# Newton's step on GpSimd, the values evicted by ScalarE, the input split one slot later, and new orders in a local-attention transformer on one core

## The chip, the cores and the metric

One NeuronCore of a Trainium2 chip runs the whole program in one launch. The metric is device time in microseconds (us): the median of three runs, and beside it one profiled execution. Engines are named as in the profile: PE (TensorE matmul), PEld (its weight loads), DVE (VectorE), ACT (ScalarE), POOL (GpSimd), SP (SyncE, which issues the DMAs).

## What is computed

The program runs two MoE phases, a recurrence, one attention with a position bias, and twice the same six-layer local transformer. The change lies in that transformer alone. Cut to what matters:

```python
def attn_layer(x, Wqkv, qs, ksc, Wo):               # x: 8 batches of 256 tokens, 128 wide
    q, k, v = split(x @ Wqkv)                       # 16 heads of 64
    q = l2norm(q) * qs;  k = l2norm(k) * ksc        # l2norm: t / max(norm(t), 1e-12)
    q = q*cos*scale + rotate_half(q)*sin*scale      # k with 1/scale
    out = local_attention(q, k, v)                  # windows of 32 tokens, looking one window back
    return out @ Wo
def ffn_layer(x, ...):                              # layer norm, 128 -> 2*341, a*gelu(gate), -> 128
for i in range(6):
    x = attn_layer(shift_tokens(x), ...) + x
    x = ffn_layer(shift_tokens(x), ...) + x
```

## The kernel before: units, slots and written-out orders

A *unit* is one batch with four of the sixteen heads; a layer has 32 units (8 batches by 4 head groups), a phase 192, the two phases 384. Every engine runs the same endless list of *slots*, one new unit per slot; in slot s it works on unit s (u0 in the code), s-1 (u1) and so on down to s-5 (u5). What an engine does inside a slot is a list written by hand (`slot(L, s)`, one per engine), and engines meet only at semaphores (`upto(engine, semaphore, unit)` waits until that unit's step is done). Buffers are mostly double, so that an engine can run ahead of another by a fraction of a slot.

The steps of a unit, with their lines: `project` (PE, L785) multiplies each of the two 128-token tiles t by the q and k weights into PSUM banks A[0], A[1], in three fp32r products each (L49 to L51); `square_of` (ACT, L979) squares a bank; `lengths` (DVE, L1111) sums squares per head; `cosine` and `sine` (DVE, L1106, L1100) do the rotation out of PSUM; `add_turned` (POOL, L1266) adds the two halves. `floor` (DVE, L1117) clamps the sums of squares; `first_guess` (ACT, L990, L993) makes a first inverse square root with Ln and Exp; `newton` (DVE, L1122, L1124, L1128) refines it in three 128x16 instructions; `normalise_qk` (POOL, L1272) applies it. `turn` (PE, L804) transposes q and k into bank TB, `take_turned` (ACT, L984) evicts them, `scores` (PE, L832), `mask_scores` (DVE, L1134), `maxima` (DVE, L1140), `exponentials` (ACT, L1002, eight of them, each followed by an accumulator read), `inverse_sums` (DVE, L1145), `normalise_weights` (POOL, L1278), `turn_weights` (PE, L844), `take_weights` (ACT, L1008), `weigh` (PE, L862), `take_output` (ACT, L1014), `merge` (PE, L876), and once in four units `update_x` (DVE, L1157). `values` (PE, L807) makes v into V_, which is the same PSUM bank as TB; `take_values` (L1151, DVE) evicts it, and SP (`spread`, L735) writes it to DRAM and reads it back as windows.

Every eighth slot starts a feed-forward chunk of two batches (`chunk(L, s, n)` is true where s-n is a multiple of 8): mean and `deviation` (13), variance (14), `normalise` (15), `high` and `low` splits (16), three gates and three `gelus` (17, with an activation table load before and after, L1039 and L1040), three linears with their `product` (17, 18, 22), `down` and `update` (23). So slots differ by s modulo 8. `next_batch` (POOL, L1242 to L1245) splits the next batch's input every fourth slot; each layer also has four weight splits (`high_group`, L596 on ACT, `low_group`, L602 on POOL) and one of the up weights.

Of the kernel before, what the change touches and what calls it, by code (L numbers as in the profile page):

```python
# [8 lines left out]
ALU = mybir.AluOpType  # L9
# [498 lines left out]
def local_transformer_phase(nc, res, d, X):  # L508
# [8 lines left out]
    with ExitStack() as ctx:  # L517
# [214 lines left out]
        with nc.Block() as block:  # L732
# [51 lines left out]
            def _(pe):  # L784
# [120 lines left out]
                def linear(c, k):  # L905
# [5 lines left out]
                    else:  # L911
                        upto_pair(pe, flog, pair(c[0], c[1] + 1), 1, 1)
# [4 lines left out]
                def down(c):  # L917
                    upto_pair(pe, fhd, c, 3, 3)
# [7 lines left out]
                def slot(L, s):  # L926
                    u0, u1, u2, u4, u5 = unit(L, s), unit(L, s - 1), unit(L, s - 2), unit(L, s - 4), unit(L, s - 5)
                    c = chunk(L, s, 17)
                    if c:
                        gate(c, 1)  # L930
                    c = chunk(L, s, 13)
                    if c:
                        mean(c)
                    if u0:
                        project(u0, 0)
                        project(u0, 1)
                    c = chunk(L, s, 17)
                    if c:
                        gate(c, 2)
                    c = chunk(L, s, 23)  # L940
                    if c:
                        down(c)
                    if u2:
                        turn(u2, 0)
                    c = chunk(L, s, 17)
                    if c:
                        linear(c, 0)
# [8 lines left out]
                    if u2:
                        turn(u2, 1)
                    if u4:
                        turn_weights(u4)
                    if u5:  # L960
                        merge(u5)
                    if u2:
                        scores(u2)
                    c = chunk(L, s, 16)
                    if c:
                        gate(c, 0)
                    if u1:
                        values(u1)
                    c = chunk(L, s, 22)
                    if c:  # L970
                        linear(c, 2)
# [3 lines left out]
            def _(act):  # L975
# [34 lines left out]

                def take_output(u):
# [813 lines left out]
```

## Time and profile before

| | us |
|---|---|
| median of three runs | 4414.74 (4410.19 to 4415.19) |
| profiled execution | 4419.39, span 4417.6 |
| DVE busy | 3447.6 (78%) |
| ACT busy | 3176.4 (72%) |
| POOL busy | 2673.5 (61%) |
| PE busy | 3899.8 (88%) |

The shares of the whole span mix phases with different limits. The two transformer phases run from about 655 to 2257 us and again in the second half of the span, and a stretch inside one of them (800 to 1853 us: 128 slots, four layers) is what the rows below are taken from. An engine overlaps the tail of one instruction with the start of the next, so the distance from start to start is shorter than the duration that a row gives.

### The profile page before, as it was taken

The page shows a single profiled execution, that of the slowest core. Times are in us where ns is not written, and L with a number is a line of the kernel's source. Part 1 is how long each engine was busy: PE and PEld are TensorE (multiplying, and loading weights), DVE is VectorE, ACT ScalarE, POOL GpSimd, SP SyncE. Part 2 cuts the span into 40 slices and gives each one's busy share as a digit, 9 for nine tenths or more (in the row PEclk, how much of TensorE's full clock was granted, in tenths as well). Part 3 has the DMA queues.
Part 4 walks back from the last instruction along what each step waited for, and adds up shares of the span by engine and source line. Part 5 has one row for each costly group of instructions (what it writes and reads, how often), then busy time and mean ns, then how long its engine had stood idle before and what let it go on. Part 6 is the DMA issues. An engine that isn't in the chain of part 4 may idle for free. (4 is left out here: it accounts for less than half of the span.)

```text
span 4417.6 us, 164417 instructions
## 1 busy us (share of the span) xinstructions
PE 3899.8 (88%) x64144; PEld 2853.1 (65%) x64144; DVE 3447.6 (78%) x6675; ACT 3176.4 (72%) x10347; POOL 2673.5 (61%) x2507
## 2 busy tenths in 40 slices
PE   7966968999999999999954896899999999999996
PEld 3423437777777777777734664777777777777773
DVE  1132129999999999999943664999999999999994
ACT  3343337888888888888841433788888888888884
POOL 1110127777777777777710332777777777877772
PEclk8987989999999999999975987999999999999997
DMA  1101113333333333333310000333333333333341
GB/s 58 57 15 44 57 47 105 115 103 119 100 116 103 106 112 108 114 97 109 117 29 0 1 0 33 103 112 104 119 99 116 104 108 112 103 117 98 106 119 37
DMA packets 549303, 377.81 MB, mean 86 GB/s; under 512 B 32576, under 2 KB 533056, under 8 KB 546240
## 3 DMA queue, kind: packets, MB, share of 16 engines
q1 hardware_dynamic: 548560, 367.57, 27.6%
q8 instruction: 507, 8.31, 0.8%
q14 instruction: 236, 1.93, 0.1%
HBM read 265.37 MB, written 102.11 MB: 83 GB/s over the span
## 5 line engine op out<-in xcount | busy, mean ns | idle before, releaser
L1266 POOL TENSOR_TENSOR lt_t<-lt_t 128x512 f32<-128x512 f32 x768 | 973.5, 1289 | 567.8 <-DVE lt_t L1100 567.8
L1002 ACT ACTIVATE lt_pb<-lt_pb,lt_mx 128x64 f32<-128x64 f32 x3072 | 1023.5, 346 | 0.0
L1272 POOL TENSOR_TENSOR lt_t<-lt_t,lt_rn 128x512 f32<-128x512 f32 x768 | 810.8, 1076 | 118.4 <-DVE lt_rn L1128 117.1
L49 PE MATMUL ps<-lt_wh,lt_xh 128*128 128x512 f32 (+1 forms) x1536 | 581.8, 379 | 148.9 <-DVE lt_t L1100 87.6
L1002 ACT ACTIVATION_READ_ACCUMULATOR lt_pb<-lt_pb,lt_mx 128x1 f32 x3072 | 610.2, 199 | 0.0
L984 ACT ACTIVATE lt_qkT<-ps 128x512 f32<-128x512 f32 x768 | 459.0, 598 | 197.2 <-PE ps L804 196.8
L1111 DVE TENSOR_REDUCE lt_ss<-lt_sq 128x8 f32<-128x512 f32 x768 | 518.7, 675 | 14.5 <-ACT lt_sq L979 9.9
L1100 DVE TENSOR_TENSOR lt_t<-ps,lt_tab 128x512 f32<-128x512 f32 x768 | 522.9, 681 | 2.9
L51 PE MATMUL ps<-lt_wh,lt_xl 128*128 128x512 f32 (+1 forms) x1536 | 523.7, 341 | 0.0
L1106 DVE TENSOR_TENSOR lt_t<-ps,lt_tab 128x512 f32<-128x512 f32 x768 | 521.6, 679 | 1.6 <-PE ps L804 0.3
L50 PE MATMUL ps<-lt_wl,lt_xh 128*128 128x512 f32 (+1 forms) x1536 | 522.8, 340 | 0.0
L804 PE MATMUL ps<-ident,lt_t 128*128 128x128 f32 x3072 | 482.8, 280 | 34.1 <-ACT lt_qkT L984 25.5
L979 ACT ACTIVATE lt_sq<-ps 128x512 f32<-128x512 f32 x768 | 452.8, 590 | 71.4 <-PE ps L51 70.5
L49 PEld LDWEIGHTS ps<-lt_wh,lt_xh 128*128 128x128 f32 x1536 | 290.5, 189 | 267.5 <-issue 150.6
L804 PEld LDWEIGHTS ps<-ident,lt_t 128*128 128x128 f32 x3072 | 355.9, 141 | 159.0 <-issue 105.6
L862 PEld LDWEIGHTS ps<-lt_pT,lt_vw 64*64 64x64 f32 x24576 | 397.1, 135 | 89.0 <-issue 88.7
L862 PE MATMUL ps<-lt_pT,lt_vw 64*64 64x32 f32 x24576 | 439.0, 221 | 4.1 <-issue 3.9
L1278 POOL TENSOR_TENSOR lt_pb<-lt_pb,lt_rd 128x512 f32<-128x512 f32 x384 | 400.8, 1044 | 34.1 <-DVE lt_rd L1145 30.7
L876 PE MATMUL ps<-lt_oT,lt_wo 128*128 128x256 f32 x1536 | 405.1, 386 | 1.8 <-ACT lt_oT L1014 1.4
L372 POOL TENSOR_TENSOR M<-M,moe_tmp 128x512 f32<-128x512 f32 x64 | 81.0, 1266 | 510.5 <-DVE moe_tmp L354 510.5
L354 DVE SCALAR_TENSOR_TENSOR moe_tmp<-ps,moe_bb,moe_cbc 128x512 f32<-128x512 f32 x64 | 48.1, 751 | 419.8 <-PE ps L306 419.8
L832 PEld LDWEIGHTS ps<-lt_qkT 64*32 64x32 f32 x24576 | 271.1, 105 | 139.1 <-issue 136.7
(196 smaller groups left out, 7989.3 us busy)
## 6 DMA issues: line engine op xcount, KB each, us to landing
lt_vw<-v_scratch SPq DMA_DIRECT2D x768, 256.0 KB, 3.7
v_scratch<-lt_vv SPq DMA_DIRECT2D x384, 256.0 KB, 2.1
lt_wraw<-in_lt_wqkv SPq DMA_DIRECT2D x56, 384.0 KB, 5.6
moe_cbc<-comb_scratch SPq DMA_DIRECT2D x16, 1024.0 KB, 6.7
moe_w<-in_moe_w SPq DMA_DIRECT2D x32, 256.0 KB, 2.8
lt_wo<-in_lt_wo SPq DMA_DIRECT2D x48, 128.0 KB, 3.7
lt_w<-in_lt_w SPq DMA_DIRECT2D x12, 341.0 KB, 4.2
lt_w<-in_lt_w SPq DMA_DIRECT2D x12, 192.0 KB, 3.3
```

Of the source, the lines that this page charges most:

```text
L49: nc.tensor.matmul(out, lh, rh, start=start, stop=False)
L50: nc.tensor.matmul(out, lh, rl, start=False, stop=False)
L51: return nc.tensor.matmul(out, ll, rh, start=False, stop=stop)
L804: ins = nc.tensor.transpose(TB[:, q * P:(q + 1) * P], t1[:, u[1] % 2, t, q * P:(q + 1) * P], ident[:, :])
L862: ins = nc.tensor.matmul(OR[r][64 * e:64 * e + 64, t * P + w * WIN:t * P + w * WIN + WIN], vw[h, k, 4 * t + w, e * DH:(e + 1) * DH], pT[h, ...
L984: nc.scalar.activation(qkT[:, u[1] % 2, :, WIN + t * P:WIN + (t + 1) * P], TB.rearrange("p (a n) -> p a n", a=4), ACT.Copy).then_inc(tE[t], 1)
L1002: ins = nc.scalar.activation(p, p, ACT.Exp, bias=mx[:, par, c:c + 1], accum_out=sm[:, par, c:c + 1])
L1100: nc.vector.tensor_tensor(o4, a4[:, :, :, ::-1, :], s4, ALU.mult).then_inc(rotd[t], 1)
L1106: nc.vector.tensor_tensor(t1[:, u[1] % 2, t, :].rearrange("p (w h c) -> p w h c", w=2, c=DH), A[t][:, :].rearrange("p (w h c) -> p w h c", ...
L1111: nc.vector.tensor_reduce(ss[:, u[1] % 2, 8 * t:8 * t + 8], sq[:, t, :].rearrange("p (h c) -> p h c", c=DH), AX.X, ALU.add).then_inc(ssd[t ...
L1266: nc.gpsimd.tensor_tensor(o, o, t2[:, t, :], ALU.add).then_inc(padd[t], 1)
L1272: nc.gpsimd.tensor_tensor(o, o, rn[:, u[1] % 2, 8 * t:8 * t + 8].unsqueeze(2).to_broadcast([P, 8, DH]), ALU.mult).then_inc(qkd[t], 1)
```

## The change

`newton` moves from DVE to POOL, as four plain 128x16 instructions (its fused subtract-and-multiply becomes two, with a new constant tile `three`). `take_values` moves from DVE to ACT. `next_batch` comes one slot later in its group of four. The orders in a slot are rewritten on PE, ACT, DVE and POOL; the steps are shifted too: tile 0 of q and k is transposed and evicted one slot earlier, `first_guess` and tile 0's and 1's `normalise_qk`, tile 1's `add_turned`, `normalise_weights`, `turn_weights` and `take_weights` stand one slot later or are split over the list, the FFN's `gate(c, 0)` moves to slot 17, `linear(c, 2)` to 21, `product(c, 1)` to 20. The turn of bank V_/TB becomes values, tile 1 of the unit before, tile 0. The core of the diff:

```diff
-                    nc.vector.tensor_tensor(ya[:, par, :], y0[:, par, :], y0[:, par, :], ALU.mult).then_inc(newt, 1)
-                    nc.vector.tensor_tensor(yb[:, par, :], ya[:, par, :], vm[:, par, :], ALU.mult).then_inc(newt, 1)
-                    nc.vector.scalar_tensor_tensor(out=rn[:, par, :], in0=yb[:, par, :], scalar=-3.0, in1=y0[:, par, :],
-                                                   op0=ALU.add, op1=ALU.mult).then_inc(rnd, 1)
+                    upto(pool, y0d, u)
+                    nc.gpsimd.tensor_tensor(ya[:, par, :], y0[:, par, :], y0[:, par, :], ALU.mult).then_inc(newt, 1)
+                    upto(pool, newt, u, 1, 3)
+                    nc.gpsimd.tensor_tensor(yb[:, par, :], ya[:, par, :], vm[:, par, :], ALU.mult).then_inc(newt, 1)
+                    upto(pool, newt, u, 2, 3)
+                    nc.gpsimd.tensor_tensor(ya[:, par, :], yb[:, par, :], res["three"][:, :], ALU.subtract).then_inc(newt, 1)
+                    upto(pool, newt, u, 3, 3)
+                    nc.gpsimd.tensor_tensor(rn[:, par, :], ya[:, par, :], y0[:, par, :], ALU.mult).then_inc(rnd, 1)
...
-                    nc.vector.tensor_copy(vv[:, u[1] % 2, :, :], V_.rearrange("p (t c) -> p t c", t=2)).then_inc(vE, 1)
+                    nc.scalar.activation(vv[:, u[1] % 2, :, :], V_.rearrange("p (t c) -> p t c", t=2), ACT.Copy).then_inc(vE, 1)
...
-                    if u[1] % GJ == 1:
-                        n = unit(u[0], u[1] - 1 + GJ)
+                    if u[1] % GJ == 2:
+                        n = unit(u[0], u[1] - 2 + GJ)
...
                     if t == 0:
-                        upto(pe, vE, u)
+                        upto(pe, tE[1], back(u, 1))
...
                     else:
-                        upto(pe, tE[0], u)
+                        upto(pe, vE, ahead(u, 1))
...
                 def values(u):
-                    upto(pe, tE[1], back(u, 1))
+                    upto(pe, tE[0], back(u, 1))
```

PE's list in a slot was: gate 1, mean, `project` of both tiles (u0), gate 2, `down`, `turn` tile 0 (u2), linears 0 and 1, `weigh` (u5), variance, `turn` tile 1 (u2), `turn_weights` (u4), `merge` (u5), `scores` (u2), gate 0, `values` (u1), linear 2. It is now: `turn_weights` (u5), `project` tile 0 (u0), `values` (u1), linear 1, `weigh` (u5), `turn` tile 1 (u2), gate 0, mean, `project` tile 1 (u0), gate 1, variance, `merge` (u5), `turn` tile 0 (u1), gate 2, linear 2, `scores` (u2), linear 0, `down`.

The orders inside one plain slot (no FFN work), each name the tile written and the tiles read. POOL before, where a unit starts at `lt_padd0` with the two products and ends with the attention weights:

```order
L1272 TENSOR_TENSOR lt_t1_8<-lt_t1_8,lt_rn_8 128x512 [waits lt_padd0_8,lt_rnd_8]
L1272 TENSOR_TENSOR lt_t1_8<-lt_t1_8,lt_rn_8 128x512 [waits lt_padd1_8,lt_rnd_8]
L1266 TENSOR_TENSOR lt_t1_8<-lt_t1_8,lt_t2_8 128x512 [waits lt_rotd0_8]
L1266 TENSOR_TENSOR lt_t1_8<-lt_t1_8,lt_t2_8 128x512 [waits lt_rotd1_8]
L1278 TENSOR_TENSOR lt_pb_8<-lt_pb_8,lt_rd_8 128x512 [waits lt_rdd_8]
```

POOL of the changed kernel, the same kind of slot (L1266 to L1272 are now Newton's step, L1278 `normalise_qk`, L1261 `add_turned`, L1284 `normalise_weights`):

```order
L1266 TENSOR_TENSOR lt_ya_8<-lt_y0_8 128x16 [waits lt_y0d_8]
L1268 TENSOR_TENSOR lt_yb_8<-lt_ya_8,lt_vm_8 128x16 [waits lt_newt_8]
L1270 TENSOR_TENSOR lt_ya_8<-lt_yb_8,three 128x16 [waits lt_newt_8]
L1272 TENSOR_TENSOR lt_rn_8<-lt_ya_8,lt_y0_8 128x16 [waits lt_newt_8]
L1278 TENSOR_TENSOR lt_t1_8<-lt_t1_8,lt_rn_8 128x512 [waits lt_padd0_8,lt_rnd_8]
L1261 TENSOR_TENSOR lt_t1_8<-lt_t1_8,lt_t2_8 128x512 [waits lt_rotd1_8]
L1284 TENSOR_TENSOR lt_pb_8<-lt_pb_8,lt_rd_8 128x512 [waits lt_rdd_8]
L1261 TENSOR_TENSOR lt_t1_8<-lt_t1_8,lt_t2_8 128x512 [waits lt_rotd0_8]
L1278 TENSOR_TENSOR lt_t1_8<-lt_t1_8,lt_rn_8 128x512 [waits lt_padd1_8,lt_rnd_8]
```

Newton's four stand at the head, each behind a wait on the one before, and the two adds are no longer neighbours. ACT before, from `first_guess` to the exponentials:

```order
L990 ACTIVATE lt_y_8<-lt_vm 128x16 [waits lt_vmd_8]
L993 ACTIVATE lt_y_8<-lt_y_8,ln 128x16 [waits lt_rnd_8,lt_lnd_8]
L979 ACTIVATE lt_sq<-ps 128x512 [waits lt_ssd0_8,lt_qkp0_8]
L984 ACTIVATE lt_qkT<-ps 128x4x128 [waits lt_simd_8,lt_tT0_8]
L979 ACTIVATE lt_sq<-ps 128x512 [waits lt_ssd1_8,lt_qkp1_8]
L1014 ACTIVATE lt_oT<-ps 128x512 [waits lt_wod_8,lt_pvd_8]
L984 ACTIVATE lt_qkT<-ps 128x4x128 [waits lt_simd_8,lt_tT1_8]
L1008 ACTIVATE lt_pT<-ps 128x512 [waits lt_pvd_8,lt_ptT_8]
L1002 ACTIVATE lt_pb,lt_sm<-lt_pb,lt_mx 128x64 [waits lt_rdd_8,lt_mxd_8]
```

ACT of the changed kernel, from the gelus of a slot 17 into the next slot (L989 `take_turned`, L1007 the second half of the exponentials, L1013 `take_weights`, L995 and L998 `first_guess`; L1020 `take_values` follows them):

```order
L1050 ACT_TABLE_LOAD [waits lt_fhd_8,lt_fg_8]
L1050 ACTIVATE lt_gl<-ps,lt_fvg 128x512 [waits lt_fvgld_8]
L1050 ACTIVATE lt_gl<-ps,lt_fvg 128x512 [waits lt_fhd_8,lt_fg_8]
L1050 ACTIVATE lt_gl<-ps,lt_fvg 85x512 [waits lt_fhd_8,lt_fg_8]
L1051 ACT_TABLE_LOAD
L989 ACTIVATE lt_qkT<-ps 128x4x128 [waits lt_simd_8,lt_tT0_8]
L1007 ACTIVATE lt_pb,lt_sm<-lt_pb,lt_mx 128x64 [waits lt_rdd_8,lt_mxd_8]
L1007 ACTIVATE lt_pb,lt_sm<-lt_pb,lt_mx 128x64 x3
L1013 ACTIVATE lt_pT<-ps 128x512 [waits lt_pvd_8,lt_ptT_8]
L995 ACTIVATE lt_y_8<-lt_vm 128x16 [waits lt_vmd_8]
L998 ACTIVATE lt_y_8<-lt_y_8,ln 128x16 [waits lt_rnd_8,lt_lnd_8]
L1020 ACTIVATE lt_vv<-ps 128x512 [waits lt_pvd_8,lt_vst_8,lt_vp_8]
```

`take_weights` now opens the slot, with `first_guess` right behind it, and the exponentials are in two halves with other work between. DVE of the changed kernel in a plain slot (L1143 maxima, L1125 lengths, L1114 sine, L1120 cosine, L1137 mask, L1132 floor, L1148 inverse sums); before, the same list also held Newton's three and the copy of the values:

```order
L1143 TENSOR_REDUCE lt_mx_8<-lt_pb_8 128x8 [waits lt_expd_8,lt_mskd_8]
L1125 TENSOR_REDUCE lt_ss_8<-lt_sq_8 128x8 [waits lt_sqd0_8]
L1114 TENSOR_TENSOR lt_t2_8<-ps,lt_tab_8 128x512 [waits lt_padd0_8,lt_sqd0_8]
L1120 TENSOR_TENSOR lt_t1_8<-ps,lt_tab_8 128x512 [waits lt_tT0_8,lt_sqd0_8]
L1125 TENSOR_REDUCE lt_ss_8<-lt_sq_8 128x8 [waits lt_sqd1_8]
L1120 TENSOR_TENSOR lt_t1_8<-ps,lt_tab_8 128x512 [waits lt_tT1_8,lt_sqd1_8]
L1137 TENSOR_TENSOR lt_pb_8<-ps,mask 128x512 [waits lt_ptT_8,lt_simd_8]
L1132 TENSOR_TENSOR lt_vm_8<-lt_ss_8,tiny 128x16 [waits lt_rnd_8,lt_ssd1_8,lt_ssd0_8]
L1114 TENSOR_TENSOR lt_t2_8<-ps,lt_tab_8 128x512 [waits lt_padd1_8,lt_sqd1_8]
L1148 RECIPROCAL lt_rd_8<-lt_sm_8 128x8 [waits lt_pnd_8,lt_expd_8]
```

Here `floor` has come to stand behind `mask_scores`, which waits for `scores`, the last PE step of a plain slot.

## Rows read from the trace of the kernel before

**Rows 1.** Windows: each engine's busy time (with its instructions) in two stretches
```profile
core 0: us, PE busy (x) PEld busy (x) DVE busy (x) ACT busy (x) POOL busy (x), PEclk, DMA share, GB/s
675.00:763.00 88.00, 81.09 (x1746) 65.58 (x1745) 85.00 (x174) 75.12 (x287) 69.66 (x68) 0.97 0.37 110
800.00:1853.00 1053.00, 999.23 (x20338) 781.30 (x20337) 1019.22 (x2010) 918.47 (x3231) 821.77 (x771) 1.00 0.37 109
```

**Rows 2.** Groups by line, 800 to 1853 us: busy, mean ns, idle before
```profile
L1151 DVE COPY lt_vv<-ps 128x512 f32<-128x512 f32 x128 | 87.3, 682 | 13.0 <-PE ps L51 12.8
...
L1124 DVE TENSOR_TENSOR lt_yb<-lt_ya,lt_vm 128x16 f32<-128x16 f32 x127 | 81.7, 643 | 4.4
...
L1122 DVE TENSOR_TENSOR lt_ya<-lt_y 128x16 f32<-128x16 f32 x127 | 60.2, 474 | 0.0
...
L1128 DVE SCALAR_TENSOR_TENSOR lt_rn<-lt_yb,lt_y 128x16 f32<-128x16 f32 x127 | 32.7, 257 | 4.4
L1117 DVE TENSOR_TENSOR lt_vm<-lt_ss,tiny 128x16 f32<-128x16 f32 x128 | 31.3, 245 | 0.0
...
L1245 POOL TENSOR_TENSOR lt_xl<-lt_xc,lt_xh 128x256 fp32r<-128x256 f32 x32 | 23.3, 730 | 2.6
```

**Rows 3.** Waits, 800 to 1853 us: total, times, longest
```profile
POOL lt_t L1266 <- DVE lt_t L1100: 189.0, 124, 2.4
ACT lt_qkT L984 <- PE ps L804: 63.6, 95, 2.3
```

**Rows 4.** Timeline of DVE and of POOL in one slot: start, duration
```profile
1529.90 0.21 DVE L1122 TENSOR_TENSOR lt_ya<-lt_y 128x16 f32<-128x16 f32 x1
1530.15 0.97 DVE L1124 TENSOR_TENSOR lt_yb<-lt_ya,lt_vm 128x16 f32<-128x16 f32 x1
...
1530.03 1.05 POOL L1278 TENSOR_TENSOR lt_pb<-lt_pb,lt_rd 128x512 f32<-128x512 f32 x1
1531.40 2.04 POOL L1272 TENSOR_TENSOR lt_t<-lt_t,lt_rn 128x512 f32<-128x512 f32 x2 [0.32 <-DVE lt_rn L1128]
1535.38 2.53 POOL L1266 TENSOR_TENSOR lt_t<-lt_t 128x512 f32<-128x512 f32 x2 [1.94 <-DVE lt_t L1100]
```

**Rows 5.** Timeline of ACT: the gelus, evictions, first and last of eight exponentials
```profile
1507.35 1.28 ACT L1040 ACT_TABLE_LOAD   x1
1509.13 0.59 ACT L984 ACTIVATE lt_qkT<-ps 128x512 f32<-128x512 f32 x1
1509.61 0.61 ACT L979 ACTIVATE lt_sq<-ps 128x512 f32<-128x512 f32 x1
...
1532.36 0.35 ACT L1002 ACTIVATE lt_pb<-lt_pb,lt_mx 128x64 f32<-128x64 f32 x1
...
1535.01 0.20 ACT L990 ACTIVATE lt_y<-lt_vm 128x16 f32<-128x16 f32 x1
1535.25 0.31 ACT L993 ACTIVATE lt_y<-lt_y,ln 128x16 f32<-128x16 f32 x1
```

**Rows 6.** Timeline of PE: `down`, then a slot's steps to the values
```profile
1551.97 2.82 PE L923 MATMUL ps<-lt_hh,lt_w 128*128 128x512 f32 x6
1554.62 0.60 PE L804 MATMUL ps<-ident,lt_t 128*128 128x128 f32 x4
...
1558.11 0.86 PE L832 MATMUL ps<-lt_qkT 64*32 64x64 f32 x64
1558.90 0.39 PE L49 MATMUL ps<-lt_wh,lt_xh 128*128 128x256 f32 x1
...
1560.79 0.40 PE L50 MATMUL ps<-lt_wl,lt_xh 128*128 128x512 f32 x1
1561.02 0.39 PE L51 MATMUL ps<-lt_wh,lt_xl 128*128 128x512 f32 x1
```

**Rows 7.** Groups by line and shape, whole span, POOL
```profile
L1266 POOL TENSOR_TENSOR lt_t<-lt_t 128x512 f32<-128x512 f32 x768 | 973.5, 1289 | 567.8 <-DVE lt_t L1100 567.8
...
L1713 POOL MEMSET tiny<- 128x16 f32 x1 | 0.1, 111 | 0.0
```

More of the change, by code:

```diff
@@ L926, in slot @@
                 def slot(L, s):
[L927 to L933, printed above, removed]
+                    u0, u1, u2, u5 = unit(L, s), unit(L, s - 1), unit(L, s - 2), unit(L, s - 5)
+                    if u5:
+                        turn_weights(u5)
                     if u0:
                         project(u0, 0)
[L936 to L947, printed above, removed]
+                    if u1:
+                        values(u1)
                     c = chunk(L, s, 18)
@@ L952, in slot @@
                         weigh(u5)
+                    if u2:
+                        turn(u2, 1)
+                    c = chunk(L, s, 17)
+                    if c:
+                        gate(c, 0)
+                    c = chunk(L, s, 13)
+                    if c:
+                        mean(c)
+                    if u0:
+                        project(u0, 1)
+                    c = chunk(L, s, 17)
+                    if c:
+                        gate(c, 1)
                     c = chunk(L, s, 14)
@@ L955, in slot @@
                         variance(c)
[L956 to L959, printed above, removed]
                     if u5:
                         merge(u5)
+                    if u1:
+                        turn(u1, 0)
+                    c = chunk(L, s, 17)
+                    if c:
+                        gate(c, 2)
+                    c = chunk(L, s, 21)
+                    if c:
+                        linear(c, 2)
                     if u2:
                         scores(u2)
-                    c = chunk(L, s, 16)
+                    c = chunk(L, s, 17)
                     if c:
[L966 to L969, printed above, removed]
+                        linear(c, 0)
+                    c = chunk(L, s, 23)
                     if c:
-                        linear(c, 2)
+                        down(c)
                 stream(pe, slot, 16)
@@ L1064, in slot @@
                         take_turned(u2, 1)
+                    c = chunk(L, s, 13)
+                    if c:
+                        square_deviation(c)
+                    if u3:
+                        exponentials(u3, 0)
+                    if u0:
+                        square_of(u0, 1)
+                    c = chunk(L, s, 17)
+                    if c:
+                        gelus(c)
                     c = chunk(L, s, 14)
@@ L1192, in slot @@
                 def slot(L, s):
[L1193 removed]
+                    u0, u2, u3, u5 = unit(L, s), unit(L, s - 2), unit(L, s - 3), unit(L, s - 5)
                     if u3:
                         maxima(u3)
[L1196 to L1197 removed]
+                    c = chunk(L, s, 22)
+                    if c:
+                        product(c, 2)
+                    if u0:
+                        lengths(u0, 0)
+                        sine(u0, 0)
+                    c = chunk(L, s, 13)
+                    if c:
+                        deviation(c)
+                    if u0:
+                        cosine(u0, 0)
+                    c = chunk(L, s, 20)
+                    if c:
+                        product(c, 1)
+                    if u0:
+                        lengths(u0, 1)
+                        cosine(u0, 1)
+                    c = chunk(L, s, 15)
+                    if c:
+                        normalise(c)
+                    if u2:
+                        mask_scores(u2)
                     c = chunk(L, s, 17)
@@ L1232, in slot @@
                         update(c)
+                    if u3:
+                        inverse_sums(u3)
+                    if u5 and u5[1] % GJ == GJ - 1:
+                        update_x(u5)
                 dve.wait_ge(fvlld, 16)
@@ L1713, in _ @@
                 nc.gpsimd.memset(tiny[:, :], 1e-24)
+                nc.gpsimd.memset(three[:, :], 3.0)
                 nc.gpsimd.memset(ln1024[:, :], float(10.0 * np.log(2.0)))
```

121 lines of the change are left out of this document (44 added, 77 removed).

## The prediction, made before the changed kernel ran

> **What bounds the kernel now.** Windows first: in 800 to 1853 us, inside a transformer phase, DVE is busy 1019 of 1053 us (97%), PE 999, ACT 918, POOL 822 [rows 1]. The stretch holds 128 slots (128 copies of the values [rows 2]), so a slot takes 8.23 us and eight of them, one period of the FFN work, 65.8. Then the waits: POOL waited 189 us for DVE's rotation products and ACT 64 us for transposes [rows 3], while nothing holds DVE for long. So DVE sets the pace, and the two phases hold 384 slots, some 3160 us of the span. PE's 95% is a modelled union; its own need is worked out below.
>
> **What leaves DVE.** Newton's three instructions hold (474 + 643 + 257) ns = 1.37 us a slot [rows 2], though alone such a one takes 0.21 [rows 4]. The reason is in the timeline: the second one, with two SBUF inputs, began at 1530.15 under a POOL instruction that ended at 1531.08, and itself ended at 1531.12 [rows 4]. Two more in this class wait for POOL in the same way. The copy of the values holds 0.68 [rows 2], 0.60 from start to start. So DVE loses about 2.0 of 7.96 busy us (1019/128) and falls to about 6.0. It is then no bound: the question is what comes next.
>
> The Trainium skill says the same in "GPSIMD Engine Reference" (section 8, Key points): GpSimd shares its SBUF interfaces with VectorE and contends with DVE instructions that have two SBUF inputs. By that rule the 128x16 `floor`, which stays on DVE, goes on paying; the trace agrees, 245 ns on average over 128 [rows 2]. The same page's section 4.1 (Engine selection) would keep elementwise work on VectorE as about twice as fast; the trace speaks against that here, since DVE paid 1.37 us for it.
>
> **What ACT gets.** From start to start an eviction or a square of 128x512 takes 0.48 us when nothing is waited for (1509.13 to 1509.61), the eight exponentials with their reads 2.65 (1532.36 to 1535.01) [rows 5]; `first_guess` about 0.45 (0.24 to its second instruction, and that one's 0.31 less the overlap). A plain slot with the values added is seven of 0.48, 2.65 and 0.45: 6.46 us. The copy at 0.48 is my value, the row of its own form and engine; it has to be made, so it can't cost less than nothing, and the DVE row, 0.68, is the upper end. ACT's other 128x512 instructions I take at the whole 0.6 of such a row, since most stand behind a wait.
>
> **What POOL gets.** No 128x16 TENSOR_TENSOR of POOL is in the trace. Below, a 128x16 memset takes 0.11 [rows 7]; above, a 128x256 TENSOR_TENSOR 0.73 [rows 2]. The 512-wide one takes 1.29 [rows 7], so the line through 256 and 512 gives 0.17 at no width and 0.20 at 16. I take 0.20, the end the line goes to, and 0.08 for each of the four hand-overs (730 ns and 2.6 us idle over 32 behind such a wait [rows 2]): 1.1 us. The ends are 0.8 and 3.2. A plain slot of POOL is two adds 2.5, two products 2.0, the weights 1.0 [rows 4] and 1.1: 6.6 us. On average POOL has 822/128 = 6.4 now [rows 1], and 7.5 then.
>
> **What PE needs.** Between 1554.62 and 1558.90 stand `turn` twice, `weigh`, `turn_weights`, `merge`, `scores`: 4.3 us. Six products of 512 columns at 0.23 (1560.79 to 1561.02) are 1.4 [rows 6], the six of 256 for the values half of that. With 0.1 for the changes of shape a plain slot is 6.5. A gate or linear is three products, 0.7; `down` is 2.65 (1551.97 to 1554.62) [rows 6], and mean and variance, each a third of its kind of work, 0.9. Per period that is 52 + 6 x 0.7 + 1.8 + 2.65 = 60.7 us.
>
> **The sum, slot by slot.** The buffers let engines drift by less than a slot, so I take for each slot modulo 8 the engine with most to do, not the average of one:
> - 0: ACT with `high`, 7.05. 1: ACT, 6.46 + two table loads of 1.28 [rows 5] + three gelus of 0.6 + 0.3 of wait, 11.2. 2: PE with linear 1, 7.2. 3 and 4: POOL, 6.6 each. 5: PE with mean and linear 2, 8.1. 6: ACT with `inverse_deviation` (two of 0.6), 7.7. 7: PE with `down`, 9.15.
> - Sum 63.6, and 0.6 for ACT's weight split, one a period (estimated from 0.48 at 512 columns for its 768, less what `down` covers): 64.2 against 65.8, 1.6 us less a period. Of the 48 periods some 44 are clear of the phases' ends: 70 us.
> - Where no FFN runs yet, at each phase's head, a slot takes 7.4 us now (88 us for 12 slots [rows 1]) and 6.6 then: 0.75 x 24 = 18 us.
> - Together 88 us, from 4419.4 to 4331 in the profiled execution, which lies 4.7 above the median: **4327 us**, 2.0% less.
>
> **What costs nothing, and its cover.** The new loop through the engines is `scores` 0.8 (1558.11 to 1558.90) [rows 6], `mask_scores` 0.6, `floor` 0.2 (up to 1.3 more if it starts under a POOL add), `first_guess` 0.5, Newton 1.1, the product 1.0, `turn` 0.5, and seven hand-overs of about 0.1: 5.4 us, up to 6.7. It stays under a slot of 8.0, so the wait of `floor` behind `mask_scores` is covered; the instructions queued behind `floor` are `sine` and `inverse_sums`, which PE and POOL need 2 us later. The three turns of bank V_/TB, all now evicted by ACT, are three evictions of 0.6, two transposes of 0.6, the values 0.7 and six hand-overs of 0.1: 4.3 us, covered too. `next_batch` (1.5 us in slots 2 and 6) is covered by POOL's free time elsewhere (7.5 of 8.0). SP's queue sees only that the values come at another moment: store and loads stay the same and have three slots until `weigh`. In slot 5 `square_deviation` stands before the exponentials and waits about 1.1 us for `deviation`, which DVE reaches only after two instructions on tile 0; PE is late there anyway.
>
> **Rivals.**
> 1. *The slots even out.* If engines drift more than I allow, the loads average: the fullest is then PE with 60.7, or ACT, now 918/128 = 7.2 [rows 1] plus 0.5: 61 us. Halfway between this and 64.2, 62.6, gives 3.2 x 44 + 18 = 159 us less: 4256; all the way 4186. For it: before, DVE stayed 97% busy through plain slots and FFN slots alike [rows 1]. Against: there one engine was far ahead of all others in load, now three lie within 0.2 us.
> 2. *Lock-step.* PE and ACT hand over to each other five times a slot (weights, output, both turned tiles, values). At 0.2 us lost a slot on top of my sum, the gain is gone: 64.2 + 1.6 = 65.8, time 4397 to 4415. For it: ACT waited 64 us for PE already when it had 13% free [rows 3, 1]. Against: DVE, which delayed the transposes then, has room now.
> 3. *POOL becomes the bound* (the other side). Newton's four stand at the head of POOL's slot, in front of everything. If one costs 0.5 us with its hand-over instead of 0.28, the four take 2.0 and POOL needs 6.4 + 2.0 = 8.4 plus 0.1 at the lumps: 8.5 x 384 against 8.23 x 384, 104 us more: 4519. It decides from 1.8 us for the four, 0.45 each. For it: the upper row, 0.73 at 256 wide, and three of four have two SBUF inputs while DVE works. Against: the line through two widths.
> 4. *The change does not relieve DVE*, since what queues behind Newton waited for other things. Rows 3 speak against it: POOL waited for DVE, not the other way.
>
> **Chances.** Forecast (4290 to 4365) 0.42; rival 1 (below 4290) 0.28; rival 2 (4365 to 4440) 0.17, of which faster 0.05, same 0.07, slower 0.05; rival 3 0.12; rival 4 0.01, at the old time. A measurement here can tell about 0.2%, 9 us. So faster 0.75, within 0.2% 0.08, slower 0.17. The range reaches from 4225 (most of rival 1) to 4440 (all of rival 2); outside are some 0.08 below and 0.10 above.
>
> **What would show it.** DVE's busy time in a like stretch near 75% with the 128x16 products gone; POOL's four at about 0.2 us each and POOL near 90%; ACT's copy at 0.6; a period of 64.2 us between `maxima` eight apart, longest in slot 1, then 7; ACT's idle time mostly before the second tile's or the output's eviction, released by PE. It is wrong if POOL's four take over 0.4 us each, if a period is under 62.5 or over 65.5, or if DVE stays above 90%.

## Result, and the profile after

| | before | after |
|---|---|---|
| median, us | 4414.97 (4410.19 to 4417.79, 4 runs) | 4717.27 (4711.67 to 4723.05, 4 runs) |
| ratio | | 1.068 (1.0663 to 1.0698) |
| profiled execution, its span | 4419.39, 4417.6 | 4711.67, 4709.9 |
| DVE / ACT busy in 800 to 1853 us | 97% / 87% | 70% / 84% |

The change costs 302 us; it comes out 390 us above the forecast of 4327 and far above its range. First the stretch of [rows 1] again, in the changed kernel (length of the stretch, then the busy time of PE, PEld, DVE, ACT, POOL with instruction counts, PE's granted clock, DMA share, GB/s):

```profile
800.00:1853.00 1053.00, 897.91 (x18578) 726.76 (x18576) 740.01 (x1367) 881.52 (x3065) 841.81 (x1168) 0.99 0.37 98
```

DVE fell from 1019 to 740 us, as meant. But nothing took its place: the busiest engine, PE, is at 85%, and the stretch now holds 116 slots of 9.08 us, where it held 128 of 8.23. Engines that are all idle by turns wait for each other. The waits of the stretch (engine, tile, line, what ended the wait: us in total, times, longest), against [rows 3]:

```profile
DVE lt_ss L1125 <- ACT lt_sq L984: 249.5, 208, 3.1
POOL lt_ya L1266 <- ACT lt_y L998: 134.1, 97, 4.0
...
PE ps L808 <- ACT lt_vv L1020: 103.6, 116, 1.2
ACT lt_vv L1020 <- PE ps L866: 100.9, 112, 1.6
...
ACT lt_pT L1013 <- PE ps L848: 23.7, 17, 2.1
```

The first two rows are large but tell of spare time: DVE and POOL wait for ACT because they have less to do. The second two are a pair that did not exist before: ACT's copy of the values (L1020) waits 101 us for PE's `weigh` (L866), nearly once a slot, and PE's next transpose (L808) waits 104 us for that copy. The copy's group in the same stretch (busy and mean ns of one, then idle before it and who ended it), and in the next fence the copy's group over the whole program, from the page:

```profile
L1020 ACT ACTIVATE lt_vv<-ps 128x512 f32<-128x512 f32 x116 | 69.2, 596 | 101.0 <-PE ps L866 100.9
```

```profile
L1020 ACT ACTIVATE lt_vv<-ps 128x512 f32<-128x512 f32 x384 | 229.1, 597 | 328.5 <-PE ps L866 324.5
```

The copy takes the 0.6 us that were forecast, but ACT stands idle 0.87 us before each (101.0/116), 328 us in all. In [rows 2] the same copy on DVE had 0.10 us of idle time before it (13.0/128), and nearly all of it ended with the last product of the values themselves (L51), not with `weigh`. One slot of ACT and of PE around it (start, duration, engine and line, in brackets the idle time before and who ended it):

```profile
1535.83 0.60 ACT L1013 ACTIVATE lt_pT<-ps 128x512 f32<-128x512 f32 x1
1536.31 0.23 ACT L995 ACTIVATE lt_y<-lt_vm 128x16 f32<-128x16 f32 x1
1536.57 0.31 ACT L998 ACTIVATE lt_y<-lt_y,ln 128x16 f32<-128x16 f32 x1
1537.81 0.60 ACT L1020 ACTIVATE lt_vv<-ps 128x512 f32<-128x512 f32 x1 [0.93 <-PE ps L866]
1538.30 0.59 ACT L984 ACTIVATE lt_sq<-ps 128x512 f32<-128x512 f32 x1
1538.78 0.61 ACT L1025 ACTIVATE lt_oT<-ps 128x512 f32<-128x512 f32 x1
1539.25 0.62 ACT L989 ACTIVATE lt_qkT<-ps 128x512 f32<-128x512 f32 x1
...
1543.34 0.59 ACT L1013 ACTIVATE lt_pT<-ps 128x512 f32<-128x512 f32 x1
```

```profile
1536.53 1.14 PE L866 MATMUL ps<-lt_pT,lt_vw 64*64 64x32 f32 x64
1538.55 0.63 PE L808 MATMUL ps<-ident,lt_t 128*128 128x128 f32 x4 [0.88 <-ACT lt_vv L1020]
```

Read it as a chain. ACT evicts the turned weights (1535.83), PE weighs with them (1536.53 to 1537.67), and only then does ACT's copy start (1537.81). The copy needs nothing that `weigh` makes. What ties it to `weigh` is a guard on a buffer: `take_values(u1)` waits `pvd` of the unit four earlier, because the values go through DRAM into `vw[u mod 4]`, which that unit's `weigh` reads. Unit u1-4 is u5, and `weigh(u5)` is the one that runs in this very slot, behind `take_weights(u5)`, which stands ahead of the copy in ACT's list, with only `first_guess` between in a plain slot. So ACT waits out a round trip through PE, and PE then waits for ACT. From 1535.83 to 1543.34 a slot is 7.51 us: 6.58 of ACT's work and 0.93 of this wait.

### The profile page after: what moved, and what is told of

It is laid out like the page before. It is cut to its first block and busy times, and to the rows that moved or that the text cites. A ratio compares the mean times of both kernels' runs of the same rounds, so it can differ in the third digit from the quotient of the medians.

```text
span 4709.9 us, 164418 instructions
## 1 busy us (share of the span) xinstructions
PE 3862.4 (82%) x64144; PEld 2903.2 (62%) x64144; DVE 2828.7 (60%) x5139; ACT 3323.7 (71%) x10731; POOL 2976.4 (63%) x4044
## 5 line engine op out<-in xcount | busy, mean ns | idle before, releaser
L1007 ACT ACTIVATE lt_pb<-lt_pb,lt_mx 128x64 f32<-128x64 f32 x3072 | 1032.1, 353 | 1.3 <-DVE lt_mx L1143 1.2
L1125 DVE TENSOR_REDUCE lt_ss<-lt_sq 128x8 f32<-128x512 f32 x768 | 526.2, 685 | 819.3 <-ACT lt_sq L984 817.2
L1261 POOL TENSOR_TENSOR lt_t<-lt_t 128x512 f32<-128x512 f32 x768 | 984.3, 1282 | 26.1 <-DVE lt_t L1120 25.6
L1278 POOL TENSOR_TENSOR lt_t<-lt_t,lt_rn 128x512 f32<-128x512 f32 x768 | 811.1, 1056 | 30.4
L808 PE MATMUL ps<-ident,lt_t 128*128 128x128 f32 x3072 | 482.5, 281 | 349.1 <-ACT lt_vv L1020 339.7
L49 PE MATMUL ps<-lt_wh,lt_xh 128*128 128x512 f32 (+1 forms) x1536 | 607.1, 395 | 62.5 <-POOL lt_xl L1240 57.2
L1007 ACT ACTIVATION_READ_ACCUMULATOR lt_pb<-lt_pb,lt_mx 128x1 f32 x3072 | 631.6, 206 | 0.0
L808 PEld LDWEIGHTS ps<-ident,lt_t 128*128 128x128 f32 x3072 | 358.8, 143 | 425.5 <-issue 370.2
L51 PE MATMUL ps<-lt_wh,lt_xl 128*128 128x512 f32 (+1 forms) x1536 | 527.6, 344 | 0.0
L1114 DVE TENSOR_TENSOR lt_t<-ps,lt_tab 128x512 f32<-128x512 f32 x768 | 523.3, 681 | 4.2
L1120 DVE TENSOR_TENSOR lt_t<-ps,lt_tab 128x512 f32<-128x512 f32 x768 | 522.6, 680 | 0.0
L866 PE MATMUL ps<-lt_pT,lt_vw 64*64 64x32 f32 x24576 | 436.0, 220 | 102.1 <-issue 64.1
L866 PEld LDWEIGHTS ps<-lt_pT,lt_vw 64*64 64x64 f32 x24576 | 402.9, 135 | 178.6 <-issue 150.2
L989 ACT ACTIVATE lt_qkT<-ps 128x512 f32<-128x512 f32 x768 | 467.4, 609 | 31.9 <-PE ps L808 31.2
L1020 ACT ACTIVATE lt_vv<-ps 128x512 f32<-128x512 f32 x384 | 229.1, 597 | 328.5 <-PE ps L866 324.5
L1284 POOL TENSOR_TENSOR lt_pb<-lt_pb,lt_rd 128x512 f32<-128x512 f32 x384 | 400.9, 1044 | 27.1 <-DVE lt_rd L1148 27.1
L1266 POOL TENSOR_TENSOR lt_ya<-lt_y 128x16 f32<-128x16 f32 x384 | 82.5, 215 | 447.3 <-ACT lt_y L998 447.3
```

Of the source, the lines that this page charges most:

```text
L49: nc.tensor.matmul(out, lh, rh, start=start, stop=False)
L51: return nc.tensor.matmul(out, ll, rh, start=False, stop=stop)
L808: ins = nc.tensor.transpose(TB[:, q * P:(q + 1) * P], t1[:, u[1] % 2, t, q * P:(q + 1) * P], ident[:, :])
L866: ins = nc.tensor.matmul(OR[r][64 * e:64 * e + 64, t * P + w * WIN:t * P + w * WIN + WIN], vw[h, k, 4 * t + w, e * DH:(e + 1) * DH], pT[h, ...
L989: nc.scalar.activation(qkT[:, u[1] % 2, :, WIN + t * P:WIN + (t + 1) * P], TB.rearrange("p (a n) -> p a n", a=4), ACT.Copy).then_inc(tE[t], 1)
L1007: ins = nc.scalar.activation(p, p, ACT.Exp, bias=mx[:, par, c:c + 1], accum_out=sm[:, par, c:c + 1])
```

## The experiments

Times are medians; the ratio is against the kernel before, timed in turns on the same chip (4411.4 to 4417.1 us), with its 95% interval. Variants are compared with each other by their medians; where they ran on different chips that is good to about 6 us, the most by which the kernel before differed between these. "Period" is the mean distance of ACT's `take_weights` eight slots apart, in phase 1 away from its ends.

### The wait for `weigh`

**The guard goes to the queue that needs it.** The write that it protects is SP's load into `vw`, not the copy into `vv`, so the wait can stand in front of that load:

```diff
  # spread (SP), behind the wait for its own store
+ upto(sp, pvd, back(u, 4))
  # take_values (ACT)
- upto(act, pvd, back(u, 4))
```

> The changed kernel with one wait moved: take_values no longer waits on ScalarE for weigh of the unit four earlier (which stands in the same slot now); SyncE waits for it in front of the two loads that need it. Theory W (this wait is the loss): ScalarE idles 101 us over 117 slots in front of the values' eviction, 0.86 us a slot; it goes, a slot falls from 9.07 to about 8.2 us, total 0.86 x 384 = 330 us less, about 4387. Rival L (three engines near full load with uneven slots is the loss, and this idle time only shows where the slack lies): the idle time moves elsewhere, under 100 us less, above 4617.

4461.78 us, ratio 1.0093 (1.0072 to 1.0114): 255 us less than the changed kernel (slot 9.08 to 8.37 us), against 330 expected and under 100 by the rival. So the wait is the greater part of the loss, and about three quarters of its 0.86 us a slot came back as time. ACT's copy now starts 0.45 us behind the second instruction of `first_guess`, and the rest of the slot moves up (6.92 us in this slot, 1532.47 to 1539.39, against 7.51). Stretch and slot as above (lines below the edit are one higher):

```profile
800.00:1853.00 1053.00, 970.10 (x20089) 783.95 (x20088) 808.88 (x1482) 956.58 (x3308) 912.54 (x1263) 0.99 0.40 106
```

```profile
1532.47 0.59 ACT L1014 ACTIVATE lt_pT<-ps 128x512 f32<-128x512 f32 x1
1532.95 0.21 ACT L996 ACTIVATE lt_y<-lt_vm 128x16 f32<-128x16 f32 x1
1533.19 0.31 ACT L999 ACTIVATE lt_y<-lt_y,ln 128x16 f32<-128x16 f32 x1
1533.64 0.60 ACT L1020 ACTIVATE lt_vv<-ps 128x512 f32<-128x512 f32 x1
...
1539.39 0.58 ACT L1014 ACTIVATE lt_pT<-ps 128x512 f32<-128x512 f32 x1
```

The control is the same edit in the kernel before:

> The kernel before with the same guard moved from VectorE to SyncE: a control. Theory R: no change, within 15 us of 4415. Rival: faster by 100 us or more.

4420.40, ratio 1.0005 (0.9991 to 1.0018). There the guard costs nothing that can be told: PE does `weigh` of that unit in the middle of its slot and makes the values at its end, so whoever has waited for the values has waited long enough for `weigh`. In the trace of the kernel before no copy waited for it. The guard has a price only at its new place.

**Work put ahead of the wait.** If only idle time were at stake, an instruction that is ready could fill it.

```diff
  # e5: ACT's slot; e6 also moves project(u0, 1) ahead of turn(u2, 1) on PE
+ square_of(u0, 0)
  take_values(u1)
- square_of(u0, 0)
```

> The changed kernel with square_of of tile 0 moved in front of take_values on ScalarE, the wait kept: a half dose. Theory W: 0.48 us of ScalarE's 0.86 to 0.93 us wait is now covered by the square, TensorE waits as before; about 0.48 x 384 = 184 us less, 4533. Rival L: within 50 us of 4717.

> The changed kernel, wait kept, with square_of of tile 0 in front of take_values on ScalarE and project of tile 1 in front of turn of tile 1 on TensorE. Theory C (weigh, the values' eviction and the transpose behind it form one chain in which ScalarE and then TensorE stand still for about 0.9 us each a slot, so covering one side alone buys nothing, as the square alone bought 29 us): with both sides covered by 0.5 to 0.7 us of work a plain slot falls from 7.5 to about 7.05, 0.45 x 384 = 170 us less, 4547. Rival S (the wait costs because SyncE's store of the values comes late): no change, 4690.

4688.09, ratio 1.0613 (1.0595 to 1.063), and 4687.30, ratio 1.0634 (1.0606 to 1.0661): 29 and 30 us less than the changed kernel, where 184 and 170 were expected. In the second one's slot the square sits in the gap, and the gap comes back in two pieces:

```profile
1535.81 0.58 ACT L1013 ACTIVATE lt_pT<-ps 128x512 f32<-128x512 f32 x1
...
1536.74 0.58 ACT L984 ACTIVATE lt_sq<-ps 128x512 f32<-128x512 f32 x1
1537.77 0.60 ACT L1020 ACTIVATE lt_vv<-ps 128x512 f32<-128x512 f32 x1 [0.44 <-PE ps L866]
1538.26 0.60 ACT L1025 ACTIVATE lt_oT<-ps 128x512 f32<-128x512 f32 x1
1539.17 0.60 ACT L989 ACTIVATE lt_qkT<-ps 128x512 f32<-128x512 f32 x1 [0.32 <-PE ps L808]
```

From the turned weights to the values it is 1.96 us here (1535.81 to 1537.77) and 1.98 in the changed kernel (1535.83 to 1537.81), and from the values to the turned q and k 1.40 (1537.77 to 1539.17) against 1.44. Over the whole stretch the medians are 1.96 against 1.97 and 1.41 against 1.45. These are two legs of a loop: through `weigh` to the copy, and through `turn` to its eviction. They kept their length when work was put beside them, so idle time beside one of them was not spare.

> The changed kernel, wait kept, with the first four exponentials in front of take_values on ScalarE, and project of tile 1 in front of turn of tile 1 on TensorE. The traces of the two half doses show the loop: take_weights, 1.96 us round TensorE's weigh to take_values, 1.40 us round turn to take_turned, then the rest of ScalarE's slot, 7.5 in all, and the square had only been taken out of the second window, which it had filled. Theory R (two round trips in series on ScalarE's queue): exponentials come from neither window, so the first is covered (0.93 + 1.32 us of work against 1.96) and the second stays full; a plain slot is then bound by TensorE, 6.6 us of work and about 0.5 of wait: 7.1 against 7.5, total 0.4 x 384 = 150 us less than 4717, 4567. Rival (the wait costs at weigh itself, whatever ScalarE does meanwhile): 4690 or more.

Four exponentials ahead of the copy (with PE's `project` ahead of `turn` too) gave 4948.61, ratio 1.1203 (1.1174 to 1.1232), 231 us worse. This was to separate the loop through ACT's queue from one through PE's alone, and it doesn't, since two new waits opened:

```profile
PE ps L808 <- ACT lt_vv L1020: 110.8, 105, 2.6
...
ACT lt_pb L1007 <- DVE lt_mx L1143: 88.8, 87, 2.2
```

The exponentials came ahead of their `maxima`, and the copy, late behind them, still held up PE's transpose. That the two legs close through ACT's queue alone is therefore read from the timelines, not shown by a run; that the guard causes the loss is shown (e1 and b1).

### The two moves apart

```diff
  # e2: Newton's three instructions back on DVE, behind maxima(u3); e10: e1 with the same
  # e4: take_values back on DVE, behind maxima(u3), with its guard
  # bN: the kernel before, and only Newton on POOL, ahead of normalise_qk(u1, 0)
  # bV: the kernel before, and only take_values on ACT, last in its slot (guard kept)
  # bNV: both of these. bNg: bNV with the guard on SP
```

> The changed kernel with Newton's three instructions back on VectorE behind maxima, everything else as changed. Theory W: VectorE has 25% and more free, GpSimd loses 1.2 us a slot, neither sets the pace: within 50 us of 4717. Rival N (GpSimd's four serial instructions at the head of its slot delay the transposes): 1.2 us a slot less at the most, 4300 to 4500.

> The variant with the guard on SyncE (4462) with Newton's step back on VectorE behind maxima. With the wait in place Newton's engine made no difference (4707 against 4717). If the new orders are bound by ScalarE and TensorE, again none: 4450 to 4475. If Newton on GpSimd matters once the wait is gone: 1.2 us a slot of GpSimd's serial chain against 1.4 of VectorE's, 4500 or 4400.

> The changed kernel with the values' eviction given back to VectorE, right behind maxima, the wait for weigh kept there. Theory W: ScalarE loses the idle time and 0.48 us of work, TensorE still waits for the eviction (0.9 us a slot) and becomes the bound with 6.5 + 0.9 in a plain slot; a slot about 8.5 us, 4500 in total. Rival L: ScalarE's load falls by 0.48 us and nothing else, 4530 at the lowest; rival V (the values on ScalarE cost nothing, Newton on GpSimd does): no change.

> The kernel before with only Newton's step moved to the head of GpSimd's slot (four instructions, 1.2 us), all other orders as before. If VectorE's load set the pace, it loses 1.4 of 8.0 us a slot and TensorE (7.6), GpSimd (7.6) and the uneven slots bound: a slot about 7.9, 0.33 x 384 = 130 us less, 4285. Rival: the serial step delays normalise_qk and the adds, and GpSimd becomes the bound in the old order: 4415 or more.

> The kernel before with only the values' eviction moved to ScalarE, at the end of its slot, where weigh of the unit four earlier is long done; its wait is kept. Theory C: no wait on weigh appears, VectorE loses 0.6 us and ScalarE gains 0.5 of 7.2: 0.4 x 384 = 150 us less, 4265. Rival: the eviction on ScalarE is dear wherever it stands, since the transposes of the next slot wait behind the exponentials for it: 4415 or more.

> The kernel before with both moves (Newton on GpSimd, values on ScalarE at the end of its slot) and all other orders as before. Newton alone gave 76 us less, the values alone 49 more. If they add: 4388. If VectorE is no bound any more after Newton has left, the values bring nothing and cost ScalarE 0.5 us: 4335 to 4400. Rival: together they free VectorE enough for 4285.

> Both moves in the old orders (4456) with the guard against weigh moved to SyncE, the edit that gave 255 us in the new orders. Here weigh of the unit four earlier is over long before the values are ready. Theory R (the wait costs only where its releaser stands just in front of it in the same slot): no change, within 15 us. Rival (the guard costs wherever it stands): 100 us and more less.

| | us | ratio (95%) | period |
|---|---|---|---|
| e2 Newton back on DVE | 4707.18 | 1.0651 (1.0633 to 1.067) | |
| e10 the same, guard on SP | 4497.03 | 1.0194 (1.0166 to 1.0223) | |
| e4 values back on DVE | 4902.80 | 1.1104 (1.1086 to 1.1123) | |
| bN Newton alone, old orders | 4335.44 | 0.9831 (0.9813 to 0.9849) | 64.19 |
| bV values alone, old orders | 4460.41 | 1.0117 (1.0097 to 1.0136) | |
| bNV both, old orders | 4456.47 | 1.0101 (1.0072 to 1.0131) | 66.68 |
| bNg both, guard on SP | 4456.67 | 1.0094 (1.0077 to 1.0111) | |
| before / after / e1 | | | 65.94 / 72.6 / 66.99 |

*Newton on GpSimd is a gain*: 76 us alone in the old orders (130 expected), 35 us (4497.03 to 4461.78) in the new ones once the guard is gone, and nothing to be told (the intervals of e2 and the changed kernel meet) while the guard sets the slot. In the best kernel that computes everything, Newton alone, PE is at 1014 of 1053 us:

```profile
800.00:1853.00 1053.00, 1014.00 (x20947) 801.68 (x20945) 912.73 (x1677) 943.55 (x3319) 956.16 (x1321) 1.00 0.41 112
```

*The values on ScalarE are a loss in the old orders*, where 4265 was expected for them alone and 4400 at the most with Newton: 49 us alone and 121 us on top of Newton (4335.44 to 4456.47). It isn't the guard there (bNg). PE's waits for the values in the stretch, with Newton alone and with both moves (one row of each kernel):

```profile
PE ps L804 <- DVE lt_vv L1140: 0.9, 4, 0.2
```

```profile
PE ps L804 <- ACT lt_vv L1015: 30.6, 74, 0.5
```

30.6 us over the stretch's 126 slots is 0.24 a slot, of the 0.31 by which the slots differ (8.02 and 8.34 us): PE, the fullest engine, now stands in every turn of the bank behind the queue of ACT, the second fullest (967 of 1053 us with both moves, where DVE has 828). That this wait makes the loss is read from the trace; no run took it away, and the copy was tried at one place only of ACT's old list. Newton alone has exactly the forecast's period, 64.2, but the forecast's copy on ACT was in it, so that agreement is chance: the sum found room for an eviction that the engines did not find.

Whether the values would be better back on DVE in the new orders without the guard's wait was not run. The variant that put them back, e4, kept the guard.

*e4 was a miss of mine*: I expected 4500, with ACT relieved and PE as the bound. It came 186 us above the changed kernel. Its trace shows the guard's wait in a third queue, and PE waiting longer for DVE than DVE for `weigh`:

```profile
POOL lt_ya L1266 <- ACT lt_y L998: 164.3, 94, 5.9
ACT lt_qkT L989 <- PE ps L808: 152.5, 128, 3.2
...
PE ps L808 <- DVE lt_vv L1146: 131.9, 110, 3.4
DVE lt_vv L1146 <- PE ps L866: 70.3, 83, 3.6
```

Here DVE waits for `weigh`, PE for DVE, and the granted clock of the stretch was 0.96, against 0.99 in the changed kernel. How the 186 us divide among these is open.

### The rest, above the forecast

With the guard gone, 135 us remain (4461.78 against 4327). The ACT waits of that kernel in the stretch:

```profile
ACT lt_pT L1014 <- PE ps L849: 31.3, 20, 2.1
...
ACT lt_sqf L1029 <- DVE lt_dev L1158: 17.1, 16, 1.6
...
ACT lt_vv L1020 <- PE ps L51: 8.9, 23, 1.5
```

**Slot 5's deviation.** The prediction priced this wait at nothing, covered by PE.

```diff
  # e7: e1, and in ACT's slot
+ exponentials(u3, 0)
  square_deviation(c)
- exponentials(u3, 0)
```

> The variant with the guard on SyncE (4462), and square_deviation moved behind the first four exponentials on ScalarE. Its trace shows ScalarE idle 1.1 us a period of eight slots in front of square_deviation (17.1 us in 16 periods). If that idle time is on the path: 1.1 x 48 = 50 us less, 4410. If TensorE with the mean and linear 2 in that slot bounds it, as the prediction had it: no change, within 12 us of 4462.

4435.13, ratio 1.0049 (1.0032 to 1.0066), 27 us less (19 by the ratios); the wait went from 17.1 us to 0.3. It was 1.07 us a period (17.1/16), the size that the prediction gave it. Were it wholly on the path, 51 us (1.07 x 48) would have gone, and none if PE covered it. What went lies between, so about half of it was covered.

**Slot 7.** The longest of ACT's waits that is left is for `turn_weights` behind `down` (e7: 35 waits, 33.1 us). Split it, cut it, or move what comes next:

```diff
  # e9: e7, and down's third product in a step of its own at the end of the next slot
+ c = chunk(L, s, 24)
+ if c:
+     down_last(c)          # DVE's update moves to 24 as well
  # e12 is e7, and bN12 is bN, with two of down's products gone
- for k, (o, n) in enumerate(DB):
+ for k, (o, n) in enumerate(DB[0:1]):
  # e13 is e12, and e14 is e7, with normalise(c) behind sine(u0, 1) and ahead of update(c) on DVE
```

> The variant at 4435 (guard on SyncE, square_deviation later), with the third of down's three products put at the end of the next slot and update with it. In its trace ScalarE waits 2.1 us a period for turn_weights, which stands behind down on TensorE. If TensorE's uneven slots are what is left: up to 0.9 to 2.0 us a period, 43 to 96 us less, 4340 to 4392. Rival (the later update holds up gate 0 and the linears instead): 4435 or more.

> The variant at 4435 (guard on SyncE, square_deviation later) with two of down's three products left out, so that only a third of the FFN's last matmul is computed. Theory T (TensorE's lump at the end of slot 7, with turn_weights right behind it, is what ScalarE waits 2.1 us for): 1.8 us of work go there, 1.5 to 2 us a period, 72 to 96 us less, 4340 to 4363. Rival A (the slots are bound by ScalarE's queue and this is slack): within 20 us of 4435.

> The kernel before with Newton on GpSimd (4335), two of down's three products left out, as in the other. Here down stands in the middle of TensorE's slot. TensorE has 7.7 of 8.0 us a slot: if that load bounds it, 1.8 x 48 = 86 us less, 4249; if VectorE, GpSimd and ScalarE bound slot 7, under 30 less, 4305 to 4335.

> The variant with two of down's products left out (4445), and normalise moved on VectorE behind floor and sine of its slot. In that variant's trace ScalarE's 1.8 us of idle time in slot 7 (waiting for turn_weights behind down) was gone, and 1.7 us had appeared one slot later in front of first_guess, which waits for floor; on VectorE floor stands behind normalise (1.8 us) and mask_scores there. Theory M (two blocks of equal length, down on TensorE and normalise on VectorE, hide each other at the step from slot 7 to 0): with both away 1.4 to 1.7 us a period go, 67 to 80 us less, 4365 to 4378. Rival A (ScalarE's queue bounds whatever stands there): above 4425.

> The variant at 4435 with down whole and normalise moved in the same way. Theory M: down alone still holds ScalarE for 1.8 us, so nothing is gained: 4420 to 4450. If VectorE's block alone were the cause: 67 to 80 us less, 4360.

In e12, e13 and bN12 two of the three products of the feed-forward's last linear map are left out. The split gave 4521.54, ratio 1.0242 (1.0218 to 1.0266), 86 us worse; the rival had named the later `update`, but what made it worse was not looked into. The others:

| | us | ratio (95%) |
|---|---|---|
| e12 `down` cut | 4444.56 | 1.0055 (1.0037 to 1.0073) |
| bN12 the same cut, Newton alone | 4298.32 | 0.9734 (0.9718 to 0.9751) |
| e13 cut, `normalise` late | 4430.15 | 1.0040 (1.0021 to 1.0058) |
| e14 `normalise` late, `down` whole | 4431.57 | 1.0033 (1.0021 to 1.0045) |

With Newton alone the cut is worth 37 us (43 by the ratios), between the 86 of PE's load as the bound and the 30 at the most of the rival: PE bounds part of that period, not all. In the changed orders it is worth nothing, and the waits say why. ACT's longest one in e7, e12 and e13 (one row of each kernel):

```profile
ACT lt_pT L1014 <- PE ps L849: 33.1, 35, 2.1
```

```profile
ACT lt_y L996 <- DVE lt_vm L1132: 34.1, 31, 2.0
```

```profile
ACT lt_rh L1041 <- DVE lt_rs L1166: 26.7, 16, 2.7
```

Take `down` away and about the same time is waited, in the same slot of the period, for DVE's `floor`: `down` and the queue in front of `floor` end at about the same time, so removing one shows the other. In e13 the wait for `floor` is gone too (6.5 us left), and again as much is waited for, by ACT's split behind `normalise` (27 us; e12 has no such wait). That one is of the experiment's own making, since it had put `normalise` later; PE's wait for the values also rose, from 15.3 to 29.5 us. So e13, at 4430 where I had expected 4365 to 4378, doesn't tell what both blocks together are worth: this stays open. e14, the same move with `down` whole, changed nothing (3.6 us less than e7), as expected.

## Why the prediction was wrong, step by step

**The step that failed** is "What costs nothing, and its cover", together with the slot's sum in "What ACT gets". The prediction checked the loops of the new order (`scores` to `turn`, and the three turns of bank V_/TB) and called both covered. It did not list the waits *inside* the moved `take_values`. One of them, `pvd` of four units back, was free at the end of DVE's slot and stands in ACT's queue right behind the step that starts the releasing one (`take_weights`, then PE's `weigh`). That made 0.87 us of idle time a slot; the period grew to 72.6, and without it 67.0. The difference, 5.6 us over 48 periods, is 269 us, against 255 measured. The diff showed this line, so it could have been seen before the run: the guard's unit (u1-4) is u5, and the order has `take_weights(u5)` ahead of it with only `first_guess` between.

The second part of the same step is the cover of the bank's turns, "4.3 us, covered too". In the old orders, where the guard costs nothing (bNg), the values on ACT took 121 us on top of Newton, and PE waited 0.24 us a slot for them. The forecast of 4327, 8 us by which Newton alone stayed above it, these 121, 5 for the new orders and 255 for the guard make up the 4717 measured, to 1 us.

Step by step:
- *DVE bounds and loses 2.0 us a slot*: right for what left it, since the durations of its instructions sum to 9.0 us a slot before and 7.0 after. Busy time is another measure: 6.4 us a slot after (740.01/116), forecast 6.0. `floor` has 0.09 of the difference; the rest is overlap that is gone, since busy time counts the overlap of neighbours once and DVE's instructions stand back to back less often now.
- *POOL at 1.1 us for Newton's four*: right. The slot's four and what follows them, in POOL's timeline:

```profile
1529.15 0.21 POOL L1266 TENSOR_TENSOR lt_ya<-lt_y 128x16 f32<-128x16 f32 x1
1529.44 0.22 POOL L1268 TENSOR_TENSOR lt_yb<-lt_ya,lt_vm 128x16 f32<-128x16 f32 x1
1529.74 0.22 POOL L1270 TENSOR_TENSOR lt_ya<-lt_yb,three 128x16 f32<-128x16 f32 x1
1530.04 0.22 POOL L1272 TENSOR_TENSOR lt_rn<-lt_ya,lt_y 128x16 f32<-128x16 f32 x1
1530.34 1.04 POOL L1278 TENSOR_TENSOR lt_t<-lt_t,lt_rn 128x512 f32<-128x512 f32 x1
```

  From the first to what follows it is 1.19 us. Rival 3 (POOL bound, 1.8 us for the four) is out.
- *`floor` goes on paying for POOL's SBUF access*: it does, and more. In the changed kernel's groups of the stretch it takes 331 ns, against 245 in [rows 2]:

```profile
L1132 DVE TENSOR_TENSOR lt_vm<-lt_ss,tiny 128x16 f32<-128x16 f32 x117 | 38.7, 331 | 0.0
```

  The single instructions say why. Before, 32 of 128 began while a POOL instruction ran; they took 486 ns on average and ended 29 to 38 ns after it. The other 96 took 157 to 170 ns. In the changed kernel 87 of 117 begin under one.

  The other rule weighed there, the Trainium skill's "GPSIMD Engine Reference", section 4.1 (Engine selection), which would keep elementwise work on VectorE, goes against the run with Newton alone: moving it away gave 76 us.
- *The copy on ACT at 0.48 us*: its duration is right (596 ns, 1537.81 to 1538.30 from start to start), its cover was not. ACT's work per period came to 60.9 us (956.58/1053 of 67.0 in e1), where the sum's slots, added up, held some 59.2; and the copy in the turns of the bank cost PE's transpose 0.24 us a slot in the old orders, also with the guard on SP (33.1 us in bNg).
- *Slot 5's deviation covered by PE*: about half wrong, 27 of 51 us came back.
- *The fullest engine of each slot, no drift*: without the guard slots 0 to 7 take 7.75, 12.03, 7.19, 7.47, 6.97, 8.77, 8.17 and 8.65 us, where the sum had 7.05, 11.2, 7.2, 6.6, 6.6, 8.1, 7.7 and 9.15. Slot 1 is the longest, as forecast; six are 0.4 to 0.9 longer, slot 2 is right, and slot 7, forecast second longest, is 0.5 shorter and comes third. In sum it is 67.0 against 64.2, and 2.8 over 48 periods is 134 us of the 135 that remain. Of these the two moves in the old orders show 121 as the price of the values on ACT; that it consists of small hand-overs, which taking the fullest engine of each slot leaves out, is my reading and not shown.
- *Rivals*: 2, the lock-step between PE and ACT, named the right pair of engines; its 0.2 us a slot was my guess at jitter, and the fixed wait is over four times that, so its upper end, 4415, was still 300 us short. Rival 1 (loads even out, below 4290) went the other way; even Newton alone stayed at 4335. Rival 4 is out: with Newton alone, relieving DVE gives 76 us.

The steps now add up from before to after by measured kernels: 4411 before; Newton on POOL -76 (4335); the values on ACT +121 (4456); the new orders, without the guard's wait, +5 (4462); the guard at its new place +255 (4717). With both moves made, then, the new orders as such bring and cost nothing (1.0094 and 1.0093 of before, both with the guard on SP). **The version that beats both kernels is Newton on GpSimd alone in the old orders: 4335.44 us, 0.9831 (0.9813 to 0.9849) of before.**

## What to carry to other kernels

When an instruction moves to another queue, all its waits move with it, the guards on buffers as well: for each, look up which step releases it and where that step now stands against it; a guard with a slot to spare in one queue can be a round trip in another. Put a guard where the dangerous write is issued (here SP's load), not with a step that only comes before it. And an engine that evicts a bank in turn with the fullest engine passes its queue on to that engine: price the hand-over, not only the copy. The guard is shown by runs; the second rule is read from the waits of bNV and bNg.

## What the runs showed of the hardware

- GpSimd took 0.215 to 0.221 us for a TENSOR_TENSOR of 128x16, 0.30 from start to start where each waits for the one before it. On DVE the three that it replaces took 0.26 to 0.64 us on average [rows 2], though 0.16 to 0.18 each where GpSimd was idle as they began: the engine that is slower at such an instruction alone was the cheaper one.
- In the trace of the kernel before (800 to 1853 us) 281 of DVE's small instructions (`floor` and Newton's three, 128x16) began while GpSimd was in an instruction, and every one of them ended 22 to 38 ns after that instruction. The 228 others took 157 to 178 ns. Newton's second one took 807 ns on average where it was held so, by nothing but where it fell.
- Filling an engine's idle time with ready work brought 29 and 30 us where 184 and 170 were expected: the round trip beside that idle time stayed at 1.96 us.
